# An attention and feed-forward layer on eight cores: the query tiles 0 to 3 move from the front of the attention loop to its end

## The reference

```python
encR = x @ R
scores = encR @ x.T                     # 4096 x 4096, causal
A = softmax(scores + mask)
x = layernorm(x + A @ x)
# feed-forward, both layers with ternary weights and 8-bit activations
h = gelu(bitlinear(x, W1, b1))          # 1024 -> 4096
x = layernorm(x + bitlinear(h, W2, b2)) # 4096 -> 1024
```

## Time and profile before

| | us |
|---|---|
| median of 2 timed executions | 2529.26 |
| lowest and highest of them | 2523.83 and 2534.69 |
| the profiled execution, slowest core | 2456.46 |
| its span, first to last instruction | 2454.9 |
| spans of the eight cores | 2432.4 to 2454.9 |

### The profile page before, as it was taken

One profiled execution on the slowest core, in us unless ns is written; L12 is line 12 of the kernel. 1 busy time (PEld: TensorE's weight loads), 2 busy tenths in 40 slices (PEclk: granted clock), 3 DMA queues, 4 the chain that ended last, 5 costly groups with the idle time before them and its releaser, 6 DMA issues.

```text
span 2454.9 us, 27480 instructions; the slowest of 8 cores (2432.4 to 2454.9 us)
## 1 busy us (share of the span) xinstructions
PE 1869.0 (76%) x9016; PEld 800.8 (33%) x9016; DVE 973.7 (40%) x1941; ACT 642.5 (26%) x1271; POOL 169.5 (7%) x303
## 2 busy tenths in 40 slices
PE   0335678885968979838999999999999899999930
PEld 0112233332423434413333333333334333333310
DVE  0042242243332323425544545454544545454422
ACT  0011122231322323213232323232332323233210
POOL 2011120011111111100000000000000000000000
PEclk9867799897989999959999999999999999999965
DMA  9677666546564554590000000000000000000038
GB/s 155 163 205 205 188 206 180 186 123 153 121 148 118 137 142 108 133 303 19 14 26 14 27 25 14 27 13 26 14 26 13 26 24 16 26 14 26 5 131 288
DMA packets 124027, 232.77 MB, mean 95 GB/s; under 512 B 52076, under 2 KB 52204, under 8 KB 122862
## 3 DMA queue, kind: packets, MB, share of 16 engines
q0 software_dynamic: 42832, 128.20, 21.2%
q1 hardware_dynamic: 66016, 88.14, 11.3%
q10 hardware_dynamic: 15040, 14.68, 2.2%
HBM read 164.11 MB, written 69.21 MB: 95 GB/s over the span
## 4 chain that ended last, share of the span: by engine, by line
PE 58%; DMA 23%; issue 7%; DVE 6%; ACT 4%; SPq 1%; POOL 1%; DVEq 0%; ACTq 0%; POOLq 0%
PE psc L752 17%; PE pav L818 9%; PE pav L822 9%; DMA bf_med<-r_bfT 6%; PE ptp L572 4%; PE psc L542 4%; DMA w1q_h<-f_big 4%; PE psc L526 4%; PE psc L758 3%; DMA w2q_h<-f_big 3%; PE pav L589 3%; DMA bf_med<-y2pre_h 3%; PE pav L595 3%; ACT bf_med L579 2%; DMA f_big<-w1t 2%
## 5 line engine op out<-in xcount | busy, mean ns | idle before, releaser
L752 PE MATMUL psc<-bf_big,bf_med 128*128 128x512 bf16 x2048 | 491.9, 383 | 6.6 <-DMA bf_big<-w1q_h 6.3
L818 PE MATMUL pav<-bf_big,bf_med 128*128 128x512 bf16 x1024 | 399.1, 390 | 1.9 <-ACT bf_med L579 1.9
L822 PE MATMUL pav<-bf_big,bf_med 128*128 128x512 bf16 x1024 | 397.8, 388 | 0.0
L526 PE MATMUL psc<-bf_big,bf_med 128*128 128x512 bf16 x512 | 159.8, 477 | 205.4 <-DMA bf_med<-r_bfT 203.7
L542 PE MATMUL psc<-bf_big,bf_med 128*128 128x512 bf16 x1152 | 285.9, 393 | 1.9 <-ACT bf_med L555 1.9
L763 ACT ACTIVATE f_big<-psc,stats 128x512 f32<-128x512 f32 x256 | 176.0, 687 | 346.2 <-PE psc L758 338.7
L767 DVE TENSOR_REDUCE stats<-f_big 128x1 f32<-128x512 f32 x256 | 169.5, 682 | 232.8 <-ACT f_big L763 232.8
L752 PEld LDWEIGHTS psc<-bf_big,bf_med 128*128 128x128 bf16 x2048 | 181.7, 98 | 239.7 <-issue 57.8
L572 PE MATMUL ptp<-ident,bf_med 128*128 128x128 bf16 x1808 | 169.9, 222 | 113.3 <-ACT bf_med L579 64.5
L555 ACT ACTIVATE bf_med<-psc,stats 128x512 bf16<-128x512 f32 x144 | 99.2, 689 | 363.1 <-PE ptp L572 183.3
L572 PEld LDWEIGHTS ptp<-ident,bf_med 128*128 128x128 bf16 x1808 | 118.3, 98 | 190.8 <-issue 159.6
(11 more groups left out here) (112 smaller groups left out, 1545.2 us busy)
## 6 DMA issues: line engine op xcount, KB each, us to landing
f_big<-w1t POOLq DMA_DIRECT2D x64, 512.0 KB, 5.8
f_big<-w2t POOLq DMA_DIRECT2D x64, 512.0 KB, 5.0
f_big<-enc POOLq DMA_DIRECT2D x32, 512.0 KB, 6.9
bf_med<-r_bfT SPq DMA_DIRECT2D x64, 256.0 KB, 4.0
y1pre_h<-f_big SPq DMA_DIRECT2D x32, 512.0 KB, 3.2
f_big<-y1pre_h POOLq DMA_DIRECT2D x32, 512.0 KB, 4.0
out<-f_big SPq DMA_DIRECT2D x32, 512.0 KB, 3.9
bf_big<-enc POOLq DMA_DIRECT2D x32, 256.0 KB, 10.5
```

The costliest lines, as they stand in the source:

```text
L526: lambda t, e=e, d=d, cur=cur, qlo=qlo, bk=bk: t.matmul(psc[bk][:, :], Rcol(cur)[:, 128 * d:128 * (d + 1)], efm(d, qlo, qlo + 512), start= ...
L752: b.op("tensor", lambda t, d=d, s4=s4, sup=sup: t.matmul(psc[s4][:, :], xq_fm[:, 128 * d:128 * (d + 1)], w1tb(d)[:, 512 * sup:512 * (sup + ...
L818: b.op("tensor", lambda t, c=c: t.matmul(pav[:, 0:512], hq_fm[:, 128 * c:128 * (c + 1)], w2tb(c)[:, 0:512], start=(c == 0), stop=False), r ...
L822: b.op("tensor", lambda t, c=c: t.matmul(pav[:, 512:1024], hq_fm[:, 128 * c:128 * (c + 1)], w2tb(c)[:, 512:1024], start=(c == 0), stop=False),
```

## The change

The order of the query tiles becomes 4, 5, ... 31, 0, 1, 2, 3, and the order of the groups for encR 1 to 7, then 0. Everything that went by the tile's number only to alternate buffers goes by the position `oi` now, and so does prep. The loads, stores and transposes of later groups are recorded at the same positions as before. In the prologue, four loads of group 0 are recorded a second time, behind the loads of R and ahead of group 1's. The diff:

```diff
         NG = NT // 4
+        SKIP = 4 if NT >= 8 else 0
+        order = list(range(SKIP, NT)) + list(range(SKIP))
+        mstream = list(range(SKIP // 4, NMAC)) + list(range(SKIP // 4))
...
+        emit_enc_loads(0)
         emit_enc_loads(1)
         emit_enc_stores(0)
         emit_enc_transp(0)
...
-        b.dma("gpsimd", eres(0), enc[0:128, :], writes=["eres0"])
+        b.dma("gpsimd", eres(0), enc[128 * order[0]:128 * (order[0] + 1), :],
+              writes=["eres0"])
...
-        def emit_encR(m):
+        def emit_encR(m, mi):
...
-                if e + 1 < 8 or m + 1 < NMAC:
+                if e + 1 < 8 or mi + 1 < NMAC:
...
-                cur = (m * 8 + e) % 2
+                cur = (mi * 8 + e) % 2
...
-        for qi in range(NT + 1):
-            nsup = (qi + 4) // 4 if qi < NT else 0
-            if qi < NT and qi % 4 == 0:
-                m = qi // 4
-                emit_encR(m)
-                emit_enc_loads(m + 4)
-                emit_enc_stores(m + 3)
-                emit_enc_transp(m + 2)
...
+        for oi in range(NT + 1):
+            qi = order[oi] if oi < NT else -1
+            nsup = (qi + 4) // 4 if oi < NT else 0
+            par = oi % 2
+            if oi < NT and oi % 4 == 0:
+                mi = oi // 4
+                emit_encR(mstream[mi], mi)
+                emit_enc_loads(mi + 4)
+                emit_enc_stores(mi + 3)
+                emit_enc_transp(mi + 2)
...
-            if qi >= 1:
-                emit_epiA(qi - 1)
-            if qi < NT:
-                emit_softmax_tail(qi)
-            if qi >= 1:
-                drain_prep((2 * qi + 1) / (2.0 * NT))
-            drain_prep((qi + 1) / (1.0 * NT))
+            if oi >= 1:
+                emit_epiA(pq, (oi - 1) % 2)
+            if oi < NT:
+                emit_softmax_tail(qi, par)
+            if oi >= 1:
+                drain_prep((2 * oi + 1) / (2.0 * NT))
+            drain_prep((oi + 1) / (1.0 * NT))
```

More of the change, by code:

```diff
@@ L533, in emit_encR, with emit_scores_super @@
                      reads=[f"psc{bk}"], writes=[f"encR{e}"])
-        def emit_scores_super(qi, sup):
+        def emit_scores_super(qi, sup, p):
             nsup = (qi + 4) // 4
@@ L538, in emit_scores_super @@
             bank = sup % 4
-            p = qi % 2
             for e in range(8):
@@ L558, in emit_scores_super, with emit_softmax_tail @@
                  reads=[f"psc{bank}", "bcn"], accum_writes=[f"A{p}", "sums4"])
-        def emit_softmax_tail(qi):
+        def emit_softmax_tail(qi, sl):
             nsup = (qi + 4) // 4
-            sl = qi % 2
             b.op("vector", lambda v, nsup=nsup, sl=sl: v.reduce_sum(
@@ L600, in emit_avM, with emit_epiA @@
                         inc=(bb == nb - 1))
-        def emit_epiA(qi):
-            sl = qi % 2
+        def emit_epiA(qi, sl):
             b.op("vector", lambda v, sl=sl: v.scalar_tensor_tensor(
@@ L625, in emit_epiA @@
                   reads=[f"y1p{sl}"], writes=[f"y1h{qi}"])
-        for qi in range(NT + 1):
-            nsup = (qi + 4) // 4 if qi < NT else 0
-            if qi < NT and qi % 4 == 0:
-                m = qi // 4
-                emit_encR(m)
-                emit_enc_loads(m + 4)
-                emit_enc_stores(m + 3)
-                emit_enc_transp(m + 2)
-            if 1 <= qi < NT:
-                b.dma("gpsimd", eres(qi % 2), enc[128 * qi:128 * (qi + 1), :],
-                      writes=[f"eres{qi % 2}"])
+        for oi in range(NT + 1):
[8 more added lines that the diff above has]
+                emit_enc_transp(mi + 2)
+            if 1 <= oi < NT:
+                b.dma("gpsimd", eres(par), enc[128 * qi:128 * (qi + 1), :],
+                      writes=[f"eres{par}"])
             ngp, groups = 0, []
-            if qi >= 1:
-                nb = qi
+            if oi >= 1:
+                pq = order[oi - 1]
+                nb = pq + 1
                 ngp = (nb + 3) // 4
@@ L643, in build_nc @@
                           for g in range(ngp)]
-                ar = f"A{(qi - 1) % 2}"
-                Ap = A_sb((qi - 1) % 2)
+                ar = f"A{(oi - 1) % 2}"
+                Ap = A_sb((oi - 1) % 2)
             for s in range(max(nsup, ngp + 1)):
                 if s < nsup:
-                    emit_scores_super(qi, s)
+                    emit_scores_super(qi, s, par)
                 if s < ngp:
@@ L651, in build_nc @@
                 if 0 <= s - 1 < ngp:
-                    emit_avM(qi - 1, groups, s - 1, s)
-            if qi >= 1:
-                emit_epiA(qi - 1)
-            if qi < NT:
-                emit_softmax_tail(qi)
-            if qi >= 1:
-                drain_prep((2 * qi + 1) / (2.0 * NT))
-            drain_prep((qi + 1) / (1.0 * NT))
+                    emit_avM(pq, groups, s - 1, s)
+            if oi >= 1:
+                emit_epiA(pq, (oi - 1) % 2)
+            if oi < NT:
+                emit_softmax_tail(qi, par)
+            if oi >= 1:
+                drain_prep((2 * oi + 1) / (2.0 * NT))
+            drain_prep((oi + 1) / (1.0 * NT))
         drain_prep(1.0)
```

## The result

The changed kernel takes 2498.42 us (median of 11 executions), the kernel before 2452.46 us (median of 10, the two that the forecast started from among them). The ratio is 1.0183, 95% interval 1.0157 to 1.0209: 45 us slower, 38 to 51. The ratio leaves out executions in which the chip ran in a disturbed, slower state, and the two early executions of before, 2524 and 2535, were such; this is why the forecast's absolute 2563 us was too high, while the level of the profiled execution, 2456, gave 2490. The forecast was +34 us. The sign was right, and the size too small by 11 us and outside the interval. The prediction took 2% (50 us) for what a measurement can tell from no change, and so gave 0.82 to "same"; the interval is 6.5 us to either side, so that a change of 34 us could have been told from none as well.

The account below looks back on a forecast made before the run. Attention was taken as bound by PE in some tiles and by a store cycle of about 30 us in second-half tiles. First sixteen positions with the start +30, second sixteen +4: +34, 2490 or 2563 us; range 2486 to 2597.

Parts of the forecast that it names:

- same: Whole kernel: no change that a measurement tells, within about 2% (50 us); chance 0.82.
- Start: +9: Prologue up to the first mask: 7 us for four more loads of enc plus 2 for score matmuls.
- +2: First mask, now of tile 4: two rounds of eight score matmuls, not one, 2 us more.
- upper bound of 14 us: Prologue: the load charge if the moved stores and transposes make R's store half as long again.
- rival C: Prologue: the start pays 14 us or more by sharing of DMA queues, 2574 as a middle; chance 0.15.
- Tiles 4 to 15 keep their prep kind and cost what they did: Attention, first sixteen positions: tiles 4 to 15 stay under first-half prep, with no time added.
- second scale step: First quantizing group, tiles 20 to 23: the weight-scale step stops PE, charged 5 us.
- m4 under cheap prep: Tiles 16 to 19 under first-half prep: 57.6 us for three tiles, 52.3 for the step into tile 20.
- m5 as first quantizing group: Tiles 20 to 23, first under second-half prep: 78 us, between 74 and upper bound 82.
- Unchanged groups: From the step into tile 24 through tiles 28 to 31: 303.3 us as before.
- m0 last: Tiles 0 to 3 at the end of attention: 175 us, three positions' prep at 30 each almost without PE work.
- rival A: Bare tiles at the end: chunks go faster, 12 save 30 us, sum +4, 2533 us; chance 0.18.

Follow-up runs that it names:

- e2: Kernel before with only the second load of group 0 added; ratio 1.0058, median 2462.1 us.
- e9: Changed kernel without the second load of group 0, run beside the changed kernel; ratio 1.0171 to the kernel before.
- e3: Kernel before with all weight preparation moved behind the last tile; ratio 1.1815.
- e4: Changed kernel with all weight preparation moved behind the last tile; ratio 1.1853 to the kernel before.
- e12: Kernel before with the sums beside attention as they were and the quantizing behind the last tile; ratio 1.1572.
- e13: Changed kernel with the sums beside attention and the quantizing behind the last tile; ratio 1.1527 to the kernel before.
- e14: Kernel before with the sums ahead of the first tile and the quantizing beside tiles 16 to 31 as it was; ratio 1.0218.
- e15: Changed kernel with the sums ahead of the first tile and the quantizing beside positions 16 to 31; ratio 1.0482 to the kernel before.
- e8: Changed kernel measured again with more rounds, nothing else altered; ratio 1.0197 to the kernel before.
- e11: Changed kernel with four staging slots and preparation spread by the tiles' PE time in its own order; ratio 0.9939 to the kernel before.
- e10: Kernel before with four staging slots and preparation spread by the tiles' PE time; ratio 0.9758.

## Why the prediction was wrong in size

The kind of mechanism was right, and terms of its sum were sized wrong, the start first of all. Step by step, as the prediction put them, each measured on the slowest core of the two profiles, whose ends of attention are 47.5 us apart (44.0 in the mean of the cores):

- **"Start: +9".** Measured +15.4: first mask at 139.59 instead of 124.19 (+14.0 in the mean of the cores, of which the second load is 12 and the rest the second round, which +2 had right). This is the step that failed by most, 6.4 us. The working charged the four loads at their spacing (7 us) and nothing to the transposes that had been moved into the flood. The profile after, e2 and e9 show that the transposes are the path: 33 us instead of 12, and SP's first column of R waits behind them in the queue, 16.2 us late. The store of R, on which the working had put the wait, is not the path. ACT's stores of R in the changed kernel:

```profile
DMA to landing us min/median/max: 2.5/2.7/35.0
```

  The longest is the last, issued at 43.69: it landed at 78.7, 1.4 us later than the last one before (48.89 + 28.4 = 77.3), and 15 us ahead of the column's issue at 93.74. Of the 16.2 us the old slack of encR took little. The upper bound of 14 us, which is also where rival C (0.15) began, was near: with it the prediction's own sum is +41. It was set aside for "the row's spacing is the nearest", though that row was one of loads and not of transposes. What the prediction cited from the Trainium skill, "DMA: Bandwidth & Descriptors", section "Queues, rings and completion order", pointed to the larger value, by a longer store of R. The trace agrees that this store takes longer, 35.0 us and not 28.4, but not that the start hangs on it; it does not show how the queues take turns.
- **"Tiles 4 to 15 keep their prep kind and cost what they did": +0.** Measured +5.0 (425.42 - 139.59 = 285.8, against 280.8), though only +2.2 in the mean of the cores. The loss is at one place: the scale step of W1 stands at a position, not at a tile. It fell behind tile 8 before, and PE had time to spare there. Now it falls behind tile 12, which PE bounds: three tiles took 52.10 us against 46.19, in the mean of the cores 52.3 against 46.3, while tiles 8 to 11 got some of it back. The row on PE:

```profile
328.70 0.19 PE L422 MATMUL psc<-stats,ones_sb 128*1 128x1 f32 x2 [4.10 <-DVE stats L420]
```

  It is the same 4 us stall as in the earlier trace rows. The prediction had charged the second scale step and forgotten the first.
- **m4 under cheap prep, 57.6 + 52.3.** Measured 57.54 + 52.41. The 0.95 us a place held.
- **m5 as first quantizing group, 78.** Measured 82.98, the upper bound. The last of its three tiles waited for prep in full (30.7 us), as it had done before; the 78 was a middle between ends and had no row behind it.
- **Unchanged groups, 303.3.** Measured 300.9.
- **m0 last, 175.** Measured 40.04 + 38.56 + 60.30 + 35.82 = 174.7: 41, 38, 30 and 30 and the closing 36 as worked out. The prediction's main claim, that the store cycle has nothing to do with PE and would stay at 30 us a tile with PE nearly idle, was right, and rival A, faster chunks in bare tiles, was wrong: the stores still land in 6 us. That it is prep's own load beside them which keeps them there, as the prediction argued, no run tests.

The three misses, 6.4 + 5.0 + 5.0, less 2.4 and 0.3 on the groups behind, are 13.7 us, which is 47.5 less the 33.8 forecast; feed-forward gave 4.0 back on these two cores. In the mean of the cores the three are 5.0, 2.2 and 3.0, so the start stays the largest. The cause was the forecast one, a trade of partners: the order of tiles costs nothing alone (e3, e4), gains with the sums (e12, e13) and loses with the quantizing (e14, e15). The parts add up in the core means, once the start is not counted twice: -8.3 less its 13.0 of start is -21.3, +59.9 less its 10.1 is +49.8, and with the 14.0 us of start of the whole change that makes 42.5 us, against 46.3 measured (e8).

One thing stays open. With four slots and even shares the gap is 46 us by the ratios and 40 by the ends of attention, and with weighted shares still 43. Of these 43, 13 are the start. The share by PE time left heavy chunks on tile 31, whose cover is no longer a long tile but encR and the scores of tile 0: in the means of the cores the four steps from tile 31's mask to tile 3's take 97.5 us in e11 and 68.1 without preparation (e4), 29 us for preparation, where the same tiles at the front of e10 take 63.5 against 54.8 (e3), 9 us. That chunks dealt in view of this cover would close the gap is not shown; I have not tried such shares.

## What to carry to other kernels

Background work that is dealt out by position is paired anew whenever the loop's order changes: write down for each iteration what it can cover and what it carries, the one-off steps too, and compare the sums, since an order that costs nothing alone can gain beside one kind of work and lose beside another. The cover of a step is the work of the iteration behind it, so short iterations belong where the background work is cheap or has run out, and not under its dearest part. An operation moved into a stretch of heavy loads is to be charged for its own slowdown there, and for all that stands behind it in its queue.

## What the runs showed of the hardware

- Eight DMA transposes of 128 x 512 took 11.9 us to issue beside two loads of R, and 33.0 us beside the stream of loads, in two kernels (the changed one and e2; 31.9 to 33.2 on all of their cores). The DMA share does not tell the two apart: it is 1.05 from 19.40 to 31.30 us before and 1.07 from 60.40 to 93.40 us after. Which part of the stream does it was not tried; without the weight loads at its end (e4) it was 27.1 to 29.6 us. Four plain stores took 6.0 to 6.4 us to issue in the same stream, against 5.2 to 5.9 ahead of it, and landed in a median of 9.0 us against 7.5. I had expected all to stretch alike.
- One more staging slot of 4 KB a partition was worth 47 us (2.0%) in the kernel before: by the order of the queue two stores can be in flight where one could. The work of DVE and of the DMA queues was unchanged.
- Twelve us in attention, on the mean of the cores, came out as 4 us of time in one pair of kernels, 6 in another and 14 in a third. The core means of the same timed executions gave 9, 8.5 and 13. A change of half a per cent on eight cores is better read from the mean of all cores than from the time of the slowest.
